# Convolution cells from a merge network beside the scores, and the sort and count cells beside the convolutions

## What is computed

```python
edge_index = jnp.stack([src, dst])       # dst is sorted, src is not
h = jnp.maximum(_layernorm(x, axis=-1), 0.0)
x = x + _L0_gnn_ref(h, ...)              # attention over edges: scores, softmax by dst, sum, Wo
x = x + _L1_gnn_ref(h, ..., edge_weight) # 5 convolutions, each with a norm over all nodes
x = x + _L2_gnn_ref(h, ...)              # gradient of a sum: additive attention, two MLPs, over edges
x = x + _L3_gnn_ref(h, ...)              # mean over neighbours, a linear layer, relu
```

## Time and profile before

| | us |
|---|---|
| median of 3 runs (11336.65 to 11345.05) | 11343.61 |
| the profiled execution, its own time | 11332.7 |
| its span | 11330.9 |
| VectorE / ScalarE / GpSimd busy | 4153.9 / 2995.9 / 6231.1 |
| TensorE busy (matmul) | 4971.7 |
| mean DMA rate | 235 GB/s |

### The profile page before, as it was taken

One profiled execution on the slowest core, in us unless ns is written; L12 is line 12 of the kernel. 1 busy time (PEld: TensorE's weight loads), 2 busy tenths in 40 slices (PEclk: granted clock), 3 DMA queues, 4 the chain that ended last, 5 costly groups with the idle time before them and its releaser, 6 DMA issues.

```text
span 11330.9 us, 88723 instructions
## 1 busy us (share of the span) xinstructions
PE 4971.7 (44%) x33461; PEld 2445.4 (22%) x33461; DVE 4153.9 (37%) x5350; ACT 2995.9 (26%) x2286; POOL 6231.1 (55%) x6250
## 2 busy tenths in 40 slices
PE   1000399800000577777556655344421530266655
PEld 0000288700000122222112121144420100112112
DVE  4555677610000000000067750088850003277730
ACT  0111100000000000000079950066630005399920
POOL 4777677767777777777770017788777660100000
PEclk5555555555555789998789986676765665599977
DMA  5666699970002999999954559755532963254568
GB/s 198 226 221 218 141 353 350 351 253 6 1 1 79 415 385 388 415 387 388 415 180 168 180 193 390 270 186 203 200 137 95 369 271 140 97 178 168 179 263 350
DMA packets 899556, 2664.78 MB, mean 235 GB/s; under 512 B 195270, under 2 KB 405303, under 8 KB 868644
## 3 DMA queue, kind: packets, MB, share of 16 engines
q1 hardware_dynamic: 670516, 2362.07, 54.6%
q0 software_dynamic: 213744, 171.80, 6.1%
q10 hardware_dynamic: 14976, 126.52, 2.7%
HBM read 1896.46 MB, written 763.47 MB: 235 GB/s over the span
## 4 chain that ended last, share of the span: by engine, by line
POOL 33%; DMA 19%; PE 14%; ACT 13%; issue 12%; ACTq 5%; DVE 3%; DVEq 1%; SPq 0%; POOLq 0%
POOL arena L416 16%; DMA arena<-cells_w 13%; POOL cells_w L419 7%; POOL xd L419 7%; ACT arena L720 6%; ACT arena L718 5%; ACTq L719 5%; PE ps L604 5%; PE ps L894 3%; DMA arena<-cells_c 3%; DMA xd<-arena 2%; POOL sorted L419 2%; PE ps L873 2%; PE ps L867 2%; ACT arena L528 1%
## 5 line engine op out<-in xcount | busy, mean ns | idle before, releaser
L604 PE MATMUL ps<-arena 128*32 128x400 f32 (+2 forms) x12200 | 2088.2, 698 | 2321.8 <-DMA arena<-cells_w 1660.4
L742 PE MATMUL ps<-arena 128*33 128x400 f32 x6400 | 1165.3, 507 | 751.6 <-DVE arena L733 751.5
L416 POOL DMA_INDIRECT arena<-t_a,arena x832 | 890.6, 1070 | 1066.3 <-DMA t_a<-arena 813.2
L604 PEld LDWEIGHTS ps<-arena 128*32 128x32 f32 (+1 forms) x12200 | 629.0, 150 | 3774.6 <-issue 2251.6
L419 POOL DMA_INDIRECT cells_t<-arena x832 | 887.1, 1066 | 291.0 <-issue 291.0
L419 POOL DMA_INDIRECT xd<-arena x832 | 872.2, 1048 | 256.3 <-issue 253.4
L419 POOL DMA_INDIRECT cells_w<-arena x832 | 809.1, 973 | 312.9 <-issue 272.1
L419 POOL DMA_INDIRECT sorted<-arena x832 | 813.7, 978 | 301.8 <-issue 287.9
L419 POOL DMA_INDIRECT cells_c<-arena x832 | 811.7, 976 | 297.1 <-issue 294.6
L416 POOL DMA_INDIRECT arena<-t_kv,idx x832 | 786.4, 945 | 257.8 <-issue 253.3
L1067 ACT ACTIVATE norm_cols<-norm_cols 128x1 f32<-128x1 f32 x5 | 1.0, 203 | 3400.1 <-DVE norm_cols L1049 3400.1
(11 more groups left out here) (467 smaller groups left out, 7437.9 us busy)
## 6 DMA issues: line engine op xcount, KB each, us to landing
arena<-cells_w SPq DMA_DIRECT2D x250, 3200.0 KB
arena<-cells_c SPq DMA_DIRECT2D x100, 3200.0 KB
cells_w<-arena SPq DMA_DIRECT2D x50, 3200.0 KB, 20.8
cells_c<-arena SPq DMA_DIRECT2D x50, 3200.0 KB
cells_t<-arena SPq DMA_DIRECT2D x50, 3200.0 KB
arena<-cells_c SPq DMA_DIRECT2D x100, 1600.0 KB, 6.5
arena<-cells_t SPq DMA_DIRECT2D x50, 3200.0 KB
arena<-cells_t SPq DMA_DIRECT2D x100, 1600.0 KB, 6.5
```

Source lines behind the costliest of these rows:

```text
L416: return pool.indirect_dma_start(dst, None, table, bass.IndirectOffsetOnAxis(ap=index, axis=0))
L604: last = pe.matmul(bank[base + k][g * f:(g + 1) * f, 0:m], own[:, t, :], TILE[b][:, g * width + at:g * width + at + m], start=t == 0, stop ...
L742: last = pe.matmul(bank[4 * kind + 2 * h + c][64 * g:64 * g + 33, 0:400], own[:, t, :], moving[:, at:at + 400], start=t == 0, stop=t == NT ...
```

## The change

- Instead of after the sort, the cells of weights are made within each partition. `local_keys_dve` makes a key for each edge: 8192 times the number of its target within the partition, plus its source. A merge network of 55 rounds (`merge_dve`) sorts 832 keys a partition (1024 with padding) and carries the weights along. 52 rounds stand in the scores' chunks, two in each after `count_dve`; 3 follow. The loop over `it` on VectorE is written out. `local_cells_dve` sums equal keys and makes the addresses, and GpSimd stores `cells_w` first, then the sort.
- The matrix keeps its layout. A target that goes on from the partition before gets a spare column (`N` + p) in place of its own, so that no two partitions store the same cell; `dense_pe` adds a 51st tile, `HOT` (one-hot rows in DRAM that say which target each partition's spare column belongs to), with the sums of the spare columns turned by TensorE (`beyond_dve`).
- `starts_dve` and `rank_dve` follow `own_made`. SyncE writes `dis` before `starts`, then the 52 fill steps, then waits for all places and loads tiles. Layers 3 to 5 use two tile buffers; their loads, `hsum`, `dh1` and `mean` are cut in pieces of 25,600 bytes in place of 6400 (`max_dma_last_dim`).
- The sort's read-back moves to ScalarE's queue after the second norm (`cells_act`). `cells_dve` stands on VectorE in layer 3, without the sum of weights; its carries go through DRAM (`CARRY`) in place of TensorE. `order_s_dve` follows `a_made`, `join_end_pool` follows `cells_t`. GpSimd's order: `cells_w`, an iota, sort, `cells_c`, `cells_t`.
- In both attentions the square of every fourth piece moves from ScalarE to VectorE (`squared_late`).

The diff, cut to its core (regions of the arena, the address arithmetic and renamed semaphores are left out):

```diff
@@ -351,11 +368,12 @@
             total += n


-        DENSE = [("gcn1", 3), ("gcn2", 3), ("gcn3", 3), ("gcn4", 3), ("gcn5", 3), ("hsum", 2), ("dh1", 2), ("mean", 3)]
+        DENSE = [("gcn1", 3, NT + 1), ("gcn2", 3, NT + 1), ("gcn3", 2, NT + 1), ("gcn4", 2, NT + 1), ("gcn5", 2, NT + 1),
+                 ("hsum", 2, NT), ("dh1", 2, NT), ("mean", 3, NT)]
         TAKES, taken = {}, [0] * TILES
@@ -585,29 +602,49 @@


         def tiles_sp(sp, name, table):
-            for t in range(NT):
-                b, n = TAKES[name][t]
+            for t, (b, n) in enumerate(TAKES[name]):
                 if n:
                     sp.wait_ge(S[f"tile_done{b}"], n)
-                sp.dma_start(TILE[b], cells(table)[:, t, 0:NR], max_dma_last_dim=NR).then_inc(S[f"tile{b}"], 16)
+                source = cells(table)[:, t, 0:NR] if t < NT else HOT
+                sp.dma_start(TILE[b], source, max_dma_last_dim=4 * NR).then_inc(S[f"tile{b}"], 16)
...
+            for t, (b, n) in enumerate(TAKES[name]):
+                if t == NT:
+                    merges = int(name[3:])
+                    pe.wait_ge(S["beyond_out"], 2 * merges - 1)
+                    pe.matmul(beyond(f)[1], carry[P - f:P, 0:P], ident[P - f:P, P - f:P], start=True, stop=True,
+                              skip_group_check=True).then_inc(S["beyond_turned"], 1)
+                    pe.wait_ge(S["beyond_out"], 2 * merges)
+                pe.wait_ge(S[f"tile{b}"], 16 * (n + 1))
+                add(TILE[b], own[:, t, :] if t < NT else spread_carry[:, 0:f], t == 0, t >= NT - 1).then_inc(S[f"tile_done{b}"], 1)
+
+        def beyond_dve(dve, layer, f):
+
+            b, n = TAKES[f"gcn{layer}"][NT - 1]
+            dve.wait_ge(S[f"tile_done{b}"], n + 1)
+            dve.tensor_copy(carry[P - f:P, 0:P], beyond(f)[0]).then_inc(S["beyond_out"], 1)
+            dve.wait_ge(S["beyond_turned"], layer)
+            dve.tensor_copy(spread_carry[:, 0:f], beyond(f)[1]).then_inc(S["beyond_out"], 1)

         def await_dense(engine, name):
-            b, n = TAKES[name][NT - 1]
+            b, n = TAKES[name][-1]
             engine.wait_ge(S[f"tile_done{b}"], n + 1)

...

+        def squared_late(b):
+
+            return b == 3
@@ -717,8 +758,10 @@
                     act.wait_ge(S["weights_used"], k - 3)
                 act.activation(groups_of(TANH[b]), piece_of(OTHER[phase], h), ACT.Tanh, bias=own[:, t:t + 1])
                 act.drain()
-                act.activation(EXPO[b], TANH[b], ACT.Exp, scale=0.5, bias=half[:])
-                act.activation(TANH[b], TANH[b], ACT.Square).then_inc(S["weights_made"], 1)
+                last = act.activation(EXPO[b], TANH[b], ACT.Exp, scale=0.5, bias=half[:])
+                if not squared_late(b):
+                    last = act.activation(TANH[b], TANH[b], ACT.Square)
+                last.then_inc(S["weights_made"], 1)

         def weigh_dve(dve, name, phase):
             for k, b, i, _, _, h in pieces(name, (phase,)):
@@ -729,6 +772,8 @@
                 last = dve.tensor_tensor(groups_of(EXPO[b]), groups_of(EXPO[b]), piece_of(PART[p], h), ALU.mult)
                 if h == 1:
                     last.then_inc(S[f"part_done{p}"], 1)
+                if squared_late(b):
+                    dve.tensor_tensor(TANH[b], TANH[b], TANH[b], ALU.mult)
                 dve.drain()
                 dve.scalar_tensor_tensor(TANH[b], TANH[b], -1.0, EXPO[b], ALU.add, ALU.mult).then_inc(S["weighed"], 1)

...
+        def network():
+
+            p = 1
+            while p < LONG:
+                k = p
+                while k >= 1:
+                    yield p, k
+                    k //= 2
+                p *= 2
+
+        def sides(buf, p, k, n):
+            blocks = buf[:, 0:n].rearrange("p (b c) -> p b c", c=2 * p)
+            if k < p:
+                blocks = blocks[:, :, k:2 * p - k]
+            pairs = blocks.rearrange("p b (g s k) -> p b g s k", s=2, k=k)
+            return pairs[:, :, :, 0, :], pairs[:, :, :, 1, :]
+
+        def merge_dve(dve, p, k):
+            n = -(-J // (2 * p)) * 2 * p
+            (ka, kb), (wa, wb) = sides(LK, p, k, n), sides(LW, p, k, n)
+            _, b, g, _ = ka.shape
+            swap, high, up, down = (a[:, 0:b * g * k].rearrange("p (b g k) -> p b g k", b=b, g=g) for a in SWAPS)
+            dve.tensor_tensor(swap, ka, kb, ALU.is_gt)
+            dve.tensor_tensor(high, ka, kb, ALU.max)
+            dve.drain()
+            dve.tensor_tensor(ka, ka, kb, ALU.min)
+            dve.tensor_tensor(up, wa, swap, ALU.mult)
+            dve.tensor_tensor(down, wb, swap, ALU.mult)
+            dve.drain()
+            dve.tensor_copy(kb, high)
+            dve.tensor_tensor(wa, wa, up, ALU.subtract)
+            dve.tensor_tensor(wb, wb, down, ALU.subtract)
+            dve.drain()
+            dve.tensor_tensor(wa, wa, down, ALU.add)
+            dve.tensor_tensor(wb, wb, up, ALU.add)
+            dve.drain()
+
+        ROUNDS = list(network())
+
+        def local_keys_dve(dve):
...
+            dve.memset(NEW[:, 0:1], 0.0)
+            dve.drain()
+            dve.tensor_tensor_scan(LK[:, 0:J], ONES_L, NEW, 0.0, ALU.mult, ALU.add)
+            dve.drain()
+            dve.scalar_tensor_tensor(LK[:, 0:J], LK[:, 0:J], float(PITCH), SRC_F, ALU.mult, ALU.add)
+            dve.drain()
+
+        def local_cells_dve(dve):
...
+            dve.tensor_tensor_scan(SUM_L, EQ_L, w, 0.0, ALU.mult, ALU.add)
...
+            dve.tensor_tensor(val_w, SUM_L, AWAY, ALU.add)
...
+            ready(dve, "w_cells_made")
+            for t in range(NT):
+                to = HOT_HALF[t * P // HALF][:, t * P % HALF:t * P % HALF + P]
+                dve.tensor_scalar(to, digits[:], float(t * P), target, ALU.add, ALU.is_equal)
+            ready(dve, "hot_made")
+
...
+        def cells_act(act):
+
+            act.wait_ge(S["sorted"], 16 * J)
+            e4 = E4.rearrange("p (j k) -> p j k", k=4)
+            part_rows = lambda a: SORTED[a:a + (EP if a < J else EP - J), :].rearrange("(p j) k -> p j k", j=J)
...
+            await_made(act, "run_ends")
+            act.dma_start(CARRY[0:3, :].rearrange("k p -> p k"), sums[:, 0:3], allow_slow_non_contiguous=True).then_inc(S["carry_moved"], 16)
+            act.wait_ge(S["carry_moved"], 16)
+            act.dma_start(CARRIES[0:1, 0:3 * P], CARRY[0:3, :].rearrange("(o k) p -> o (k p)", o=1)).then_inc(S["carry_moved"], 16)
+            await_made(act, "carries_made")
+            act.dma_start(CARRY[3:4, :], CARRIES[0:1, 5 * P:6 * P]).then_inc(S["carry_moved"], 16)
+            act.wait_ge(S["carry_moved"], 16 * 3)
+            act.dma_start(sums[:, 4:5], CARRY[3:4, :].rearrange("o p -> p o"), allow_slow_non_contiguous=True).then_inc(S["carry_moved"], 16)
...
             ready(dve, "iota_kept")
...
             dve.memset(carry[:, 0:HEADS], -BIG)
             dve.drain()
-            with dve.Fori(0, IT) as it:
+            for it in range(IT):
                 for b in range(2):
                     W4 = HEADS * CJ
                     tie, raw, step, shift = (T[:, i * W4:(i + 1) * W4] for i in range(4))
@@ -1236,6 +1383,8 @@
                     heads = lambda a: a.rearrange("p (h j) -> p h j", h=HEADS)
                     parts = lambda a: a.rearrange("p (h k j) -> p h k j", h=HEADS, k=DH + 1)
                     count_dve(dve, it, b)
+                    for p, k in ROUNDS[4 * it + 2 * b:4 * it + 2 * b + 2]:
+                        merge_dve(dve, p, k)
                     dve.wait_ge(S[f"rows{b}"], it * (16 * CJ) + 16 * CJ)
                     await_prepared(dve, "scores", it, b)
@@ -1289,8 +1438,9 @@
             scores_ends_dve(dve)


-            starts_dve(dve)
-            rank_dve(dve)
+            for p, k in ROUNDS[4 * IT:]:
+                merge_dve(dve, p, k)
+            local_cells_dve(dve)


...
             dve.tensor_tensor(nodes(OWN, 32), h, over(dis[:], 32), ALU.mult)
             ready(dve, "own_made")
-            cells_dve(dve)
-            order_s_dve(dve)
+
+            dve.wait_ge(S["hot_kept"], 32)
+            starts_dve(dve)
+            rank_dve(dve)


             dve.wait_ge(S["dis_read"], 16 * 6)
             for layer, f in GCN.items():
+                if layer == 3:
+                    cells_dve(dve)
+                beyond_dve(dve, layer, f)
                 await_dense(dve, f"gcn{layer}")
                 if layer == 1:
@@ -1400,6 +1555,7 @@
                                          A_BIAS.unsqueeze(1).broadcast_to([P, got.shape[1], 64]), ALU.add)
             product_dve(dve, "A", split_a, P)
             ready(dve, "a_made")
+            order_s_dve(dve)
             await_dense(dve, "hsum")
             dve.wait_ge(S["a2_kept"], 16)
...
             await_made(act, "join_shifts")
             act.activation(sums[:, 20:32], sums[:, 8:20], ACT.Exp).then_inc(S["join_scales"], 1)
-            rank_act(act)
             await_made(act, "degree")
```

(48 more changed lines are left out.)

258 lines of the change are left out of this document (142 added, 116 removed).

## The result

The changed kernel takes **11019.14 us** (median of 4 runs, 11005.25 to 11030.64); the kernel before took 11344.33 in the same comparison (11336.65 to 11347.83, 4 runs). The ratio is 0.9714, with a 95% interval of 0.9697 to 0.9731. It is faster, by 325 us, where 554 were forecast, and 99 us above the range.

The account below looks back on a forecast made before the run. GpSimd's passes set the time before 3627, the DMA engines in the convolutions. 11332.7 - 491 (gather of `t_a` earlier) - 60 (attention on the way back) = 10782, against the median 10,790; range 10,560 to 10,920.

Parts of the forecast that it names:

- The step that failed: Convolutions' tile loads: wider pieces priced at nothing, gain or loss bounded by 5% (20 us on the last 400 us pass).
- Rival (d): Sort beside the convolutions: stores at 1.69 us each, not 1.33, ending 300 us later; total 11,090; chance 0.05.
- The scores: Scores pass: merge rounds hidden on VectorE but delaying GpSimd's gathers, +48 us over 26 chunks (bounds 0 and 100).
- First store of `cells_w`: GpSimd after the scores: this store starts at 1446 in place of 2544.7.
- The gap from sort to `cells_c`: From last sort store to first store of cells: 52 us (40 to 90), with read-back and four DRAM trips.
- `cells_t` beside the attention: GpSimd's stores during the first attention: one per VectorE instruction, 2.0 us each; the pass ends at 6231.
- Start of the convolutions: Tile loads follow the fills in the sync queue, so convolutions start at 2610 in place of 3627.
- Their end: Five convolutions: 420 us each for layers 1 and 2, 510 each for layers 3 to 5, ending at 4980.
- The tail: After the gather of `t_a`: attention on the way back 60 us shorter, the edge pass following.
- (a): First attention: stores not held up, `cells_t` ends at 5920, gather of `t_a` at 6008; total 10,565; chance 0.13.
- (b): Convolutions late: with two buffers layers 3 to 5 take 600 us each, gather at 6280; total 10,835; chance 0.12.
- (c): Scores pass: merge rounds become the bound, kernel slower than before; 11,370 at 20.5 us a round; chance 0.02.

Follow-up runs that it names:

- experiment 1: The changed kernel with tile loads in pieces of 6400 bytes again, all else as changed: 10761.46 us, ratio 0.9492.
- Experiment 3: The kernel before the change, with only its tile loads widened to pieces of 25,600 bytes: 11347.6 us, ratio 1.0013.
- experiment 8: Against experiment 1, every 1600-column VectorE instruction of the first attention cut in two (800 columns): 10757.15 us, ratio 0.9488.

## Why the forecast was right in kind and wrong in size

**What held.** The bound is what was named: GpSimd's passes one after another, the 813 us of idle time gone, the gather of `t_a` started by the end of `cells_t`. With the one edit taken back, in experiment 1, the gather of `t_a` comes out at 6230.6 for 6236 and the time at 10,761 for 10,790 (smaller misses, below, cancel in part).

**The step that failed** is in the paragraph on the convolutions: "The wider pieces of the loads (25,600 bytes in place of 6,400) I price at nothing: the engines are at 0.99 already, so a gain is bounded by 5%, and so is a loss." That bounded what the pieces do to the tile loads, and there it was right: the convolutions end at the same time with either. It didn't ask what they do to the *other* transfers on those engines. That loss was 258 us by the medians (238 by the profiled spans): against experiment 1, 173 in the sort, 62 in the edge pass, 14 in `cells_c` and `cells_t`. What the runs showed in place of "nothing": the wide pieces delay the landing of GpSimd's stores, and GpSimd waits for that landing after every 113 stores (25 to 58 us in four of the sort's seven pauses, not 3 to 7) and at line 2117 in the edge pass. The row for the sort's pace, `cells_c` at 1.33 us a store, was measured beside narrow pieces, and so was not a price for stores beside wide ones.

**Rival (d)**, "its stores are slow under the tile loads", is what happened, in part: 1.54 us a store instead of the 1.69 that it supposed, and 171 us instead of 300. It had 0.05 of the chance, on the ground that `cells_c` kept its pace there; the diff held the reason why that row didn't carry over. Experiment 3 shows it directly: with that edit alone `cells_c` took 306 us more in the kernel before, 303 of them in its seven pauses.

**The other terms.** The scores: +48 foretold, 32 measured (gathers over 1071.1 us against 1038.7 before), inside the bounds; the estimate of half an instruction's length a gather was somewhat dear, and its mechanism (a transfer waits out whatever is running) was too coarse, as experiment 8 shows. First store of `cells_w`: 18 early. The gap from sort to `cells_c`: 52 foretold (40 to 90), 70 measured and 73 without wide pieces. The last read-back, line 1146, holds ScalarE's queue for 19.8 us (18.8 in experiment 1), and each of the four transfers of the carries takes 5 to 10 us:

```profile
3835.91 19.83 ACTq L1146 DMA_DIRECT2D arena<-sorted  x1
...
3870.75 0.40 ACTq L1150 DMA_DIRECT2D carry_rows<-sums  x1
...
3880.35 0.23 ACTq L1152 DMA_DIRECT2D arena<-carry_rows  x1
...
3888.44 0.22 ACTq L1154 DMA_DIRECT2D carry_rows<-arena  x1
```

`cells_t` beside the attention: 2.0 us a store foretold, 1.90 measured (experiment 1), by the rule that was used, one store for each long instruction of VectorE; the added squares were not counted as places where stores get through, and they are. Start of the convolutions: 2610 foretold, 2590. Their end: 4980 foretold; with either piece the last tile of cells was issued near 4854, the last one-hot tile at 4864. Of the difference some 20 us are the earlier start, some 20 layers 1 and 2, the rest the layers with two buffers: 10.0 and 9.5 us a tile in layers 3 and 4, as foretold (9.8), but 8.8 in layer 5. It didn't matter: in experiment 1 the loads of the attention ended near 5781 and `cells_t` at 6222. The tail: -60 foretold; the attention on the way back gave 64, and "the edge pass follows" was wrong by 59 (wide `dh1` loads; 1384 us without them).

**Rivals (a), (b), (c).** (a), stores not held up in the attention, fell: 2.29, 1.90, 1.88 and 1.53 us a store followed the number and length of VectorE's instructions of the same stage. The Trainium skill (SBUF — State Buffer, "Who interferes with whom") infers that `tensor_tensor` doesn't stall descriptor generation. The prediction held the 2.1 us a store against that; the runs don't bear this out. They agree with the rule of the same section that the prediction quotes, that such an instruction with two SBUF inputs holds up a later GpSimd instruction that reads SBUF, but only at a store's beginning: its last 0.84 us run on beside instructions of that kind (experiment 8). Which part of a store writes descriptors no run shows, so the inference is neither proved nor refuted. (b) fell: in experiment 1 the attention's last load was issued at 5781.5, 449 us ahead of the gather, and the chain through the convolutions had room. (c) fell too: a round takes 5 to 6 us, as estimated (5.3), and not 20.

**What stays open.** That GpSimd waits for the landing of its stores after every 113 is shown, by the packet counts; why after 113 is not. Nor is it shown why whole-row pieces delay these packets when pieces of half a row do not, and why only with a third tile in flight. Ahead of the first pause 97 of 113 stores' packets were moved with pieces of 25,600 bytes, and 110 with 12,800 or with 6400. By what order the DMA engines served the queues is not seen.
